# Turning x on VectorE in 32x32 blocks, and centring the weights instead of x

## The chip, the cores and the metric

The kernel runs on one core of a Trainium2 chip. The metric is device microseconds for one execution. TensorE does matmuls and transposes into PSUM, VectorE (DVE) and ScalarE (ACT) move and combine what stands there, GpSimd (POOL) does some elementwise work in SBUF, and SyncE (SP) issues most DMAs, one after the other from one queue.

## What is computed

The reference, cut to what matters here; x is 4 x 1024 x 2048, the context 4 x 64 x 2048, everything float32:

```
h   = layernorm(x)
Q   = h @ Wq.T + bq ;  K = ctx @ Wk.T + bk
att = softmax(Q @ K.T / sqrt(2048)) @ ctx
x1  = x + tanh(g_xattn) * att
h2  = layernorm(x1)
q   = h2 @ fWq.T                               # 64 wide
w   = softmax over the 8 best of 512 slots     # scores of q with aux_keys
aux = (w @ aux_values) @ Wvd.T @ Wvu.T
u   = uncertainty(h2)                          # gelu(h2 @ Wu1.T + bu1) @ Wu2.T, variance, mean log
out = x1 + tanh(g_ffn) * (h2 + gate(u) * aux)
```

## The kernel before

The 4096 tokens are 32 tiles of 128 (8 per batch). Every product in full precision is three matmuls over a high part (rounded to fp32r, made by ScalarE) and a low part (the rest, made by VectorE): `split_product`, lines 46 to 48. The kernel is a row of blocks, each with its own instruction list for every engine; a barrier of the engines stands between blocks.

- `keys_block` (0 to 139.5 us): TensorE turns the context and each of 16 row tiles of Wk (`transpose_group`, line 76: four 128x128 transposes into one PSUM bank), ScalarE and VectorE make high and low parts, 48 matmuls of 256 columns give one tile of the keys' transpose. In the last round the first piece of Wq is converted (lines 222 and 265).
- `score_weights_block` (139.5 to 258.5 us): the score weights are Wq transposed times the keys. For each of 16 column tiles n of Wq, a load brings the 16 pieces of 128 columns of all rows (`load_wq`, two buffers), lines 372 and 402 make the parts, 48 matmuls sum over the rows of Wq into one bank (5.76 us), lines 380 and 409 split the result, and SP stores it. SP alternates loads and stores. Meanwhile POOL subtracts the context's row means (lines 359 and 361), and ScalarE and VectorE split that (390, 417).
- `ffn_block` (258.5 to 304.2 us): 11 jobs turn Wvd, Wvu, the aux values, fWq and the four row tiles of Wu1, and two products are made in between (at jobs 4 and 8). ScalarE takes the jobs' high parts in order (line 596).
- `token_block` (304.2 to about 1021 us): first two context products, then the loop over tiles. x of tile t is loaded (`load_x`), VectorE takes its moments (`bn_stats`, line 1125), ScalarE subtracts the mean (line 958), TensorE turns it in four groups (`turn_x`, line 824), ScalarE and VectorE make the parts xT (lines 963 and 1135). TensorE multiplies xT by the "b" weights (320 columns: 128 of the batch's scores and covariance, 64 of fWq, 128 of Wu1), then by 384 columns of Wu1, then adds the attention's part (lines 911 and 912), which ends a tile.
- `output_block`: loads x again, adds attention and memory parts, and stores. It is bound by its transfers.

The order of the work in the loop is written out by hand, in the function `tile` of each engine; every engine works on the rest of tile t-1 ("late"), on tile t, and on the preparation of tile t+1. On TensorE: b part with the query's transpose of t-1 in its middle, routing scores of t-1, the 384-column part in quarters with the four groups of transposes of x of t+1, the attention's transpose and the slots' transposes between them, slot values, and the attention's part. On VectorE: `late_stats` and `late_scale` (t-1, ends with the hidden layer, line 1185), `late_q_lo`, `late_poly`, scores and softmax of t, `late_slots` (t-1), the low parts of x of t+1 with the moments of t+2 between them, `late_z`. On SP: one load of x per tile, into two buffers; every 8 tiles, after the load of tile 8b+1, it waits for the b part of tile 8b-1 (`S["b_sum"]`), loads the batch's joined b weights (`load_joined_b`, two DMAs of 1 MB into the only buffer), waits for that tile's end and loads the batch's context weights. TensorE waits for the joined weights (`b_in`) at the start of a batch.

```
            with sp.Fori(1, BATCH) as b:
                for k in range(8):
                    sp.wait_ge(S["turned"], G * (8 * b + k - 1))
                    load_x(sp, io, x, x_in, 8 * b + k, k % 2)
                    if k == 1:
                        sp.wait_ge(S["b_sum"], 8 * b)
                        load_joined_b(sp, scr, keep, b)
```

## Time and profile before

| | |
|---|---|
| median of 3 runs | 1194.56 us (1188.38 to 1195.55) |
| profiled execution | 1195.68 us, span 1193.8 us |
| mean granted TensorE clock | 0.971 |
| TensorE matmuls | 1121.9 us busy (94%) |
| VectorE | 749.2 us (63%) |
| ScalarE | 453.6 us (38%) |
| GpSimd | 189.4 us (16%) |
| DMA | 185.28 MB, mean 155 GB/s |

The span runs from the first to the last instruction. Busy time of TensorE counts overlapping matmuls once; its ends are modelled. A wait is put down to the instruction whose semaphore came last. "PEclk" is the share of full clock that was granted.

### The profile page before, as it was taken

To read this page: it belongs to the slowest core of one execution; us is meant where nothing else is said; L and a number is where in the kernel's file an instruction comes from. 1 tells how busy PE (TensorE), PEld (TensorE's weight loads), DVE (VectorE), ACT (ScalarE), POOL (GpSimd) and SP (SyncE) were. 2 spreads that over 40 slices of the span, in tenths; PEclk is the share of its full clock that TensorE was granted. 3 is DMA by queue.
4 is the path that set the end of the run, shared out by engine and by line. 5 is a ranking of instruction groups with operands and counts; after the bars stand their busy time and mean duration, and the time that the engine had idled before them with its cause. 6 is when DMAs were issued, how large, how long until landed. Compare 5 with 4: busy or idle time off the path is not lost. (4 is left out here: it accounts for less than half of the span.)

```text
span 1193.8 us, 21180 instructions
## 1 busy us (share of the span) xinstructions
PE 1121.9 (94%) x7402; PEld 1068.1 (89%) x7402; DVE 749.2 (63%) x1886; ACT 453.6 (38%) x743; POOL 189.4 (16%) x277
## 2 busy tenths in 40 slices
PE   7999889899899999999999999999999994599998
PEld 6999789887899999999999999999999993488886
DVE  6555665446426676767666666667676756777776
ACT  3333314335214343333343343433343423444554
POOL 0000330000001212121212121212222223500000
PEclk9999979899999999999999999999999996799999
DMA  7333449786427711320102320103111117689999
GB/s 282 127 139 138 125 135 303 211 286 268 106 88 195 202 39 67 106 87 35 70 35 70 122 70 35 70 35 121 71 66 40 52 54 167 254 303 390 427 427 390
DMA packets 114647, 185.28 MB, mean 155 GB/s; under 512 B 45876, under 2 KB 95060, under 8 KB 97624
## 3 DMA queue, kind: packets, MB, share of 16 engines
q1 hardware_dynamic: 109432, 147.11, 37.3%
q10 hardware_dynamic: 4608, 33.56, 6.7%
q0 software_dynamic: 576, 4.19, 0.8%
q8 instruction: 19, 0.31, 0.1%
q14 instruction: 12, 0.10, 0.0%
HBM read 140.55 MB, written 54.79 MB: 164 GB/s over the span
## 5 line engine op out<-in xcount | busy, mean ns | idle before, releaser
L46 PE MATMUL tk_hidden_sum<-b_weights,k_turned 128*128 128x384 f32 x512 | 180.0, 352 | 0.0
L48 PE MATMUL tk_hidden_sum<-b_weights,k_turned 128*128 128x384 f32 x512 | 172.4, 337 | 0.0
L47 PE MATMUL tk_hidden_sum<-b_weights,k_turned 128*128 128x384 f32 x512 | 171.5, 335 | 0.0
L46 PE MATMUL tk_b_sum<-b_weights,k_turned 128*128 128x320 f32 (+1 forms) x528 | 166.3, 315 | 0.0
L48 PE MATMUL tk_b_sum<-b_weights,k_turned 128*128 128x320 f32 (+1 forms) x528 | 163.8, 310 | 0.0
L47 PE MATMUL tk_b_sum<-b_weights,k_turned 128*128 128x320 f32 (+1 forms) x528 | 163.4, 309 | 0.0
L963 ACT ACTIVATE k_turned<-tk_bank 128x512 fp32r<-128x512 f32 x128 | 76.5, 598 | 203.0 <-PE tk_bank L76 185.2
L1135 DVE TENSOR_TENSOR k_turned<-tk_bank,k_turned 128x512 fp32r<-128x512 f32 x128 | 88.3, 691 | 66.2 <-ACT k_turned L963 65.8
L46 PEld LDWEIGHTS tk_b_sum<-b_weights,k_turned 128*128 128x128 f32 x528 | 99.2, 188 | 0.3
L47 PEld LDWEIGHTS tk_b_sum<-b_weights,k_turned 128*128 128x128 f32 x528 | 99.3, 188 | 0.0
L48 PEld LDWEIGHTS tk_b_sum<-b_weights,k_turned 128*128 128x128 f32 x528 | 99.1, 188 | 0.0
L47 PEld LDWEIGHTS tk_hidden_sum<-b_weights,k_turned 128*128 128x128 f32 x512 | 96.6, 189 | 1.4
L46 PEld LDWEIGHTS tk_hidden_sum<-b_weights,k_turned 128*128 128x128 f32 x512 | 96.4, 188 | 1.4
L48 PEld LDWEIGHTS tk_hidden_sum<-b_weights,k_turned 128*128 128x128 f32 x512 | 96.1, 188 | 0.0
L46 PE MATMUL sw_mt<-a_KT,a_T 128*128 128x256 f32 x256 | 76.6, 299 | 17.5 <-DVE a_T L402 8.6
L1125 DVE BATCH_NORM_STATS2 tk_stats<-k_rows 128x6 f32<-128x512 f32 x128 | 81.6, 681 | 2.1 <-DMA k_rows<-in_x_dram 2.1
L402 DVE TENSOR_TENSOR a_T<-k_rows,a_T 128x1024 fp32r<-128x1024 f32 x30 | 51.9, 1772 | 48.6 <-ACT a_T L372 48.6
L76 PE MATMUL tk_bank<-k_ident,k_rows 128*128 128x128 f32 x512 | 76.5, 272 | 1.4 <-DVE k_turned L1135 1.4
L46 PE MATMUL ky_keys<-k_turned,a_T 128*128 128x256 f32 x256 | 77.4, 302 | 0.1
L1481 DVE TENSOR_TENSOR k_rows<-k_rows,ob_out 128x512 f32<-128x512 f32 x88 | 59.7, 686 | 27.5 <-PE ob_out L48 23.7
L47 PE MATMUL sw_mt<-a_KT,a_T 128*128 128x256 f32 x256 | 75.8, 296 | 0.0
L48 PE MATMUL sw_mt<-a_KT,a_T 128*128 128x256 f32 x256 | 75.6, 295 | 0.0
(263 smaller groups left out, 2613.2 us busy)
## 6 DMA issues: line engine op xcount, KB each, us to landing
k_rows<-in_x_dram SPq DMA_DIRECT2D x54, 1024.0 KB, 4.9
out_dram<-k_rows ACTq DMA_DIRECT2D x22, 1024.0 KB, 10.6
k_rows<-in_Wk_dram SPq DMA_DIRECT2D x16, 1024.0 KB, 4.8
k_rows<-in_Wq_dram SPq DMA_DIRECT2D x16, 1024.0 KB, 6.5
ob_x<-in_x_dram SPq DMA_DIRECT2D x10, 1024.0 KB, 11.3
out_dram<-ob_x ACTq DMA_DIRECT2D x10, 1024.0 KB, 10.4
b_weights<-scratch_b SPq DMA_DIRECT2D x6, 1024.0 KB, 6.9
scratch_mt<-k_way_out SPq DMA_DIRECT2D x32, 128.0 KB, 2.6
```

The lines of the kernel that those rows point to most:

```text
L46: pe.matmul(out, lh, rh, start=start, stop=False, skip_group_check=skip)
L47: pe.matmul(out, lh, rl, start=False, stop=False, skip_group_check=skip)
L48: return pe.matmul(out, ll, rh, start=False, stop=stop, skip_group_check=skip)
L76: ins = pe.transpose(bank[:, k * rows:(k + 1) * rows], src[0:rows, c * P:(c + 1) * P], ident[0:rows, 0:rows])
L402: dve.tensor_tensor(half(T[u][1], h), half(wq_rows[u], h), f32(half(T[u][0], h)), ALU.subtract).then_inc(lo_done, 1)
L963: act.activation(xT[u][0][:, 4 * g:4 * g + 4, :], bank[g % 2][:].rearrange("p (k n) -> p k n", k=4), ACT.Copy).then_inc(S["x_hi"], 1)
L1125: dve.bn_stats(stats[:, k, :], x[u][:, k * QN:(k + 1) * QN])
L1135: dve.tensor_tensor(xT[u][1][:, 4 * g:4 * g + 4, :], bank[g % 2][:].rearrange("p (k n) -> p k n", k=4), f32(xT[u][0][:, 4 * g:4 * g + 4, : ...
L1481: dve.tensor_tensor(x[s][:, cols], x[s][:, cols], po[n][:], ALU.add).then_inc(S["added"], 1)
```

## The change

- x is no longer centred and no longer turned on TensorE. Every tile is loaded twice: plain (`load_rows`) for the moments, and in blocks (`load_blocks`, four DMAs): partitions 32q to 32q+31 get the columns of quarter q of the rows, four rows of the tile to a partition. VectorE's block transpose then writes four chunks of xT into a PSUM bank, in which row p of chunk c is feature 16p + c. It reads with a step of 16 floats.
- So that this fits, all other operands take the same order of features: the transposes of the context, Wk, fWq and Wu1 on TensorE read every 16th column (`spread=True`).
- To make up for x not being centred, the weights' rows are: for Wq a sum on ScalarE, the negated mean on VectorE, and the mean added in the conversions; for the five jobs of fWq and Wu1 three more ScalarE operations with two drains (`centre`).
- The score weights are made with the loops exchanged: each of 16 row tiles of Wq is loaded whole, with three buffers, and its 48 matmuls add to all 16 results, which stand in the 8 banks of PSUM. All results are split and stored at the end, 4 MB in eight DMAs. `ffn_block` waits for these stores before job 4, since its weights take that memory.
- In the loop, VectorE gets the four block transposes, ScalarE loses the centring, the moments of t+1 instead of t+2 come behind the low parts, and SP waits for the moments of tile t-1 before it loads tile t plainly.

The core of the diff (lines of plumbing, memory and the last tiles left out):

```diff
-def transpose_group(pe, bank, src, g, ident, rows=P):
+def transpose_group(pe, bank, src, g, ident, rows=P, spread=False):
 
     for k in range(4):
         c = 4 * g + k
-        ins = pe.transpose(bank[:, k * rows:(k + 1) * rows], src[0:rows, c * P:(c + 1) * P],
-                           ident[0:rows, 0:rows])
+        part = slice(c, D, KC) if spread else slice(c * P, (c + 1) * P)
+        ins = pe.transpose(bank[:, k * rows:(k + 1) * rows], src[0:rows, part], ident[0:rows, 0:rows])
     return ins
+
+
+def spread(rows):
+
+    return rows.rearrange("p (n c) -> p c n", c=KC)
...
+def wq_slot(n):
+
+    return (2, 0, 1)[n % WQ_RING]
+
+
+def load_wq(sp, io, keep, n):
+
+    sp.dma_start(keep["rows"][wq_slot(n)][:], io["Wq"][n * P:(n + 1) * P, :]).then_inc(keep["wq_in"][n % WQ_RING], 16)
+
+
+def wq_sum(act, keep, n):
+
+    rows = keep["rows"][wq_slot(n)]
+    act.wait_ge(keep["wq_in"][n % WQ_RING], 16 * (n // WQ_RING + 1))
+    return act.activation(rows[:], rows[:], ACT.Copy, accum_out=keep["wq_sum"][:, n:n + 1])
+
+
+def wq_negative_mean(dve, keep, n):
+
+    return dve.tensor_scalar(keep["wq_nmean"][:, n:n + 1], keep["wq_sum"][:, n:n + 1], -1.0 / D, None, ALU.mult)
+
+
+def wq_high(act, keep, n, own):
+
+    return act.activation(keep["T"][n % 2][0][:, own, :], spread(keep["rows"][wq_slot(n)][:])[:, own, :],
+                          ACT.Identity, bias=keep["wq_nmean"][:, n:n + 1])
+
+
+def wq_low(dve, keep, n, own):
+
+    hi, lo = keep["T"][n % 2]
+    return dve.scalar_tensor_tensor(lo[:, own, :], spread(keep["rows"][wq_slot(n)][:])[:, own, :],
+                                    keep["wq_nmean"][:, n:n + 1], f32(hi[:, own, :]), ALU.add, ALU.subtract)
...
+            load_ffn(sp, io, rows, keep["ffn_in"], 0)
+            for n in range(WQ_RING, KC):
+                if n > WQ_RING:
+                    sp.wait_ge(lo_done, 2 * (n - WQ_RING))
+                load_wq(sp, io, keep, n)
+            for n in range(1, FFN_RING):
+                sp.wait_ge(lo_done, 2 * (KC - FFN_RING + n))
+                load_ffn(sp, io, rows, keep["ffn_in"], n)
+            for k in range(KC // 4):
+                sp.wait_ge(out_lo, 2 * k + 2)
                 for part in range(2):
-                    sp.dma_start(scr["mt"][part, :, bass.ds(n, 1), :].rearrange("p o n -> p (o n)"),
-                                 f32(out[u][part])).then_inc(stored[u], 16)
-
-            def body(j, first=False):
-                for u in range(2):
-                    n = 2 * j + u
-                    if not (first and u == 0):
-                        sp.wait_ge(lo_done, 2 * (n - 2))
-                    load_wq(sp, io, rows, rows_in, n, u)
-                    if not (first and u == 0):
-                        store(n - 3, 1 - u)
-
-            body(1, first=True)
-            with sp.Fori(2, KC // 2) as j:
-                body(j)
-
-            for n in range(2):
-                load_ffn(sp, io, rows, keep["ffn_in"], n)
-            store(KC - 3, 1)
-            for u in range(2):
-                sp.wait_ge(lo_done, 2 * (KC - 2 + u))
-                load_ffn(sp, io, rows, keep["ffn_in"], 2 + u)
-                store(KC - 2 + u, u)
+                    sp.dma_start(scr["mt"][part, :, 4 * k:4 * k + 4, :],
+                                 f32(out[part][:, 4 * k:4 * k + 4, :])).then_inc(keep["mt_out"], 16)
...
+            row_sum(1)
+            for n in range(1, KC):
+                if n + 1 < KC:
+                    row_sum(n + 1)
+                weights_hi(n)
...
+            def step(n, u, first=False, last=False):
+                for c in range(KC):
+                    if c % (KC // 2) == 0 and not first:
+                        pe.wait_ge(lo_done, 2 * (n - 1) + c // (KC // 2) + 1)
+                    ins = split_product(pe, bank[c // 2][:, (c % 2) * CR:(c % 2 + 1) * CR],
+                                        (T[u][0][:, c, :], T[u][1][:, c, :]),
+                                        (at(KT[0], n), at(KT[1], n)), first and c % 2 == 0, last, True)
+                    if last and c % 2 == 1:
+                        ins.then_inc(product, 1)
+                if not last:
+                    ins.then_inc(used, 1)
...
+            def centre(n):
+
+                own, r = rows[ffn_buffer(n)], jobs[n][0]
+                act.wait_ge(rows_in[ffn_buffer(n)], 16 * (n // FFN_RING + 1))
+                act.activation(own[0:r, :], own[0:r, :], ACT.Copy, accum_out=row_sum[0:r, :])
+                act.drain()
+                act.activation(row_nmean[0:r, :], row_sum[0:r, :], ACT.Copy, scale=-1.0 / D)
+                act.drain()
+                act.activation(own[0:r, :], own[0:r, :], ACT.Identity,
+                               bias=row_nmean[0:r, 0:1]).then_inc(centred, 1)
+
             for n, (r, dst) in enumerate(jobs):
+                if n + 1 in CENTRED_JOBS:
+                    centre(n + 1)
                 if n == WVU:
                     continue
+                if n == CENTRED_JOBS[0]:
+                    act.wait_ge(keep["mt_out"], MT_STORED)
...
+def load_blocks(sp, io, keep, t):
+
+
+    view = io["x"].rearrange("(t k j) (q f) -> t q j k f", k=P // LANES, j=LANES, q=QUADS)
+    for q in range(QUADS):
+        sp.dma_start(keep["blocks"][q * LANES:(q + 1) * LANES, :].rearrange("j (k f) -> j k f", f=QN),
+                     view[bass.ds(t, 1), q].rearrange("o j k f -> (o j) k f")).then_inc(keep["blocks_in"], 16)
+
+
+def load_rows(sp, io, keep, t):
+
+    sp.dma_start(keep["plain"][:], io["x"].rearrange("(t p) d -> t p d", p=P)[bass.ds(t, 1)]
+                 .rearrange("o p d -> p (o d)")).then_inc(keep["plain_in"], 16)
...
+        def load_tile(sp, t):
+            sp.wait_ge(S["turned"], G * t)
+            load_blocks(sp, io, keep, t)
+            sp.wait_ge(S["mean_var"], t)
+            load_rows(sp, io, keep, t)
...
             with sp.Fori(1, BATCH) as b:
                 for k in range(8):
-                    sp.wait_ge(S["turned"], G * (8 * b + k - 1))
-                    load_x(sp, io, x, x_in, 8 * b + k, k % 2)
+                    load_tile(sp, 8 * b + k)
                     if k == 1:
...
+            def tile(t, u, late=True, late_first=False, last=False):
                 if late:
                     late_square(t - 1)
+                if not last:
+                    x_hi(t + 1, 1 - u, 0)
+                    x_hi(t + 1, 1 - u, 1)
+                if late:
                     late_q_hi(t - 1, late_first)
+                if not last:
+                    x_hi(t + 1, 1 - u, 2)
+                    x_hi(t + 1, 1 - u, 3)
                 soft(t)
                 if late:
                     late_tanh(t - 1)
-                if not last:
-                    x_hi(t + 1, 1 - u, 0)
-                if late:
                     late_exp(t - 1)
-                if not last:
-                    x_hi(t + 1, 1 - u, 1)
                 att_hi(t)
-                if not last:
-                    x_hi(t + 1, 1 - u, 2)
                 if late:
                     late_w_out(t - 1, late_first)
...
+            def turn_x(t, g):
+                dve.transpose(bank[g % 2][:].rearrange("p (c k j) -> p c k j", c=4, j=LANES),
+                              blocks[:].rearrange("p (k i c) -> p c k i", k=P // LANES, c=KC)[:, 4 * g:4 * g + 4]
+                              ).then_inc(S["turned"], 1)
...
+            def tile(t, u, j, late=True, last=False, first=False, second=False):
                 if late:
                     late_stats(t - 1, 1 - u, (j if u else j - 1) // 4, second)
                     late_scale(t - 1, 1 - u)
+                if not last:
+                    turn_ready(t + 1)
+                    turn_x(t + 1, 0)
+                    turn_x(t + 1, 1)
+                if late:
                     late_q_lo(t - 1)
                     late_poly(t - 1)
+                if not last:
+                    x_lo(t + 1, 1 - u, 0)
+                    x_lo(t + 1, 1 - u, 1)
+                    dve.drain()
+                    turn_x(t + 1, 2)
+                    turn_x(t + 1, 3)
                 soft_scores(t, u, j // 4)
                 soft_att(t, u, first or second)
                 if late:
                     late_slots(t - 1)
                 if not last:
-                    x_lo(t + 1, 1 - u, 0)
-                    x_lo(t + 1, 1 - u, 1)
+                    x_lo(t + 1, 1 - u, 2)
+                    x_lo(t + 1, 1 - u, 3)
                 att_lo(t)
                 if late:
                     late_learned(t - 1, 1 - u)
-                if ahead:
-                    moments_of(u, j + 1, (0, 1))
                 if not last:
-                    x_lo(t + 1, 1 - u, 2)
-                if ahead:
-                    moments_of(u, j + 1, (2, 3))
-                    moments(u)
-                if not last:
-                    x_lo(t + 1, 1 - u, 3)
+                    moments(t + 1, 1 - u)
                 if late:
                     late_z(t - 1)
```

## Rows read from the trace of the kernel before

**Rows 1.** Windows: stretch, us, busy of PE, PEld, DVE, ACT, POOL, clock, DMA share, GB/s.

```profile
139.50:258.50 119.00, 100.99 (x768) 99.74 (x768) 62.06 (x49) 38.25 (x48) 21.08 (x6) 0.90 0.71 225
349.00:992.50 643.50, 643.41 (x4254) 633.45 (x4253) 418.44 (x1281) 239.63 (x469) 139.00 (x247) 1.00 0.25 78
1060.00:1193.80 133.80, 128.64 (x590) 105.01 (x588) 100.76 (x239) 63.85 (x52) 0.00 (x0) 1.00 0.99 406
```

**Rows 2.** Timeline of PE, one tile of the loop: start, us, line, operation, count.

```profile
700.55 0.60 PE L76 MATMUL tk_bank<-k_ident,k_rows 128*128 128x128 f32 x4
...
720.62 0.34 PE L48 MATMUL tk_hidden_sum<-b_weights,k_turned 128*128 128x384 f32 x1
720.79 0.60 PE L76 MATMUL tk_bank<-k_ident,k_rows 128*128 128x128 f32 x4
721.14 0.42 PE L46 MATMUL tk_hidden_sum<-b_weights,k_turned 128*128 128x384 f32 x1
721.40 0.34 PE L47 MATMUL tk_hidden_sum<-b_weights,k_turned 128*128 128x384 f32 x1
```

**Rows 3.** Waits of DVE over eight tiles: line, releaser, us, times, longest.

```profile
DVE k_rows L1145 <- PE tk_b_sum L48: 16.5, 8, 2.2
DVE k_turned L1135 <- ACT k_turned L963: 10.8, 16, 1.2
DVE tk_query_stack L1190 <- ACT c_query_ones L980: 8.5, 8, 1.1
DVE k_rows L1180 <- POOL tk_stats L1064: 5.3, 8, 0.7
DVE tk_exp_inv L1152 <- ACT k_rows L968: 4.1, 8, 0.5
```

**Rows 4.** Timeline of DVE in the loop: two moments, one scalar operation.

```profile
706.03 1.28 DVE L1125 BATCH_NORM_STATS2 tk_stats<-k_rows 128x6 f32<-128x512 f32 x2
...
715.62 0.43 DVE L1195 TENSOR_SCALAR k_rows<-k_rows 128x512 f32<-128x512 f32 x1
```

**Rows 5.** Line L1229 (a helper): durations in ns, minimum, median, maximum.

```profile
L1229 DVE TENSOR_TENSOR k_rows<-k_rows x6: 191/192/193, 1008.7 to 1018.9; 128x32 f32<-128x32 f32 x6
...
L1229 DVE TENSOR_TENSOR k_rows<-k_rows,k_stats x2: 214/216/217, 1007.6 to 1020.1; 128x32 f32<-128x32 f32 x2
```

**Rows 6.** Page, groups: line, shapes, count, busy us, mean ns, idle before.

```profile
L963 ACT ACTIVATE k_turned<-tk_bank 128x512 fp32r<-128x512 f32 x128 | 76.5, 598 | 203.0 <-PE tk_bank L76 185.2
```

**Rows 7.** Timeline of SP, issues of the last batch's joined weights.

```profile
819.30 2.06 SPq L673 DMA_DIRECT2D b_weights<-scratch_b  x2
```

**Rows 8.** DMA busy tenths, 40 slices of 0.3 us from 819 us.

```profile
DMA  0000016999999999999999999993111000000000
```

**Rows 9.** Windows of two steps of the score weights, columns as in the first.

```profile
214.80:223.40 8.60, 8.54 (x50) 8.55 (x51) 2.69 (x3) 2.07 (x3) 0.00 (x0) 0.66 0.80 229
223.40:229.10 5.70, 5.70 (x50) 5.70 (x50) 2.70 (x3) 2.27 (x3) 0.00 (x0) 1.00 0.51 158
```

**Rows 10.** Waits of PE, 195 to 262 us.

```profile
PE sw_mt L46 <- DVE k_way_out L409: 8.0, 2, 7.5
```

**Rows 11.** Timeline of ACT, end of the keys stage.

```profile
133.49 1.90 ACT L222 ACTIVATE a_T<-k_rows 128x2048 fp32r<-128x2048 f32 x1
```

**Rows 12.** Timeline of DVE, end of the keys, start of the score weights.

```profile
135.41 2.29 DVE L265 TENSOR_TENSOR a_T<-k_rows,a_T 128x2048 fp32r<-128x2048 f32 x1 [1.36 <-ACT a_T L222]
...
141.27 21.17 DVE L402 TENSOR_TENSOR a_T<-k_rows,a_T 128x1024 fp32r<-128x1024 f32 x4 [1.37 <-ACT a_T L372]
```

**Rows 13.** Timeline of PE: transposes with 64 moving columns.

```profile
270.46 0.64 PE L76 MATMUL fw_bank<-k_ident,k_rows 64*128 64x64 f32 x7
```

**Rows 14.** Groups of ACT in the score-weights stage.

```profile
L372 ACT ACTIVATE a_T<-k_rows 128x1024 fp32r<-128x1024 f32 x30 | 30.1, 1051 | 72.7 <-DMA k_rows<-in_Wq_dram 44.2 <-PE sw_mt L48 26.9 <-PEq L84 1.6
```

**Rows 15.** Timeline of ACT, FFN weights: idle before, releaser.

```profile
280.31 4.46 ACT L596 ACTIVATE b_weights<-fw_bank 128x512 fp32r<-128x512 f32 x8 [7.63 <-PE fw_bank L76]
...
295.03 4.46 ACT L596 ACTIVATE b_weights<-fw_bank 128x512 fp32r<-128x512 f32 x8 [5.43 <-PE fw_av L48]
```

More of the change, by code:

```diff
@@ L374, in step @@
-            def step(n, u, j, first=False, ahead=True):
-                act.wait_ge(product, n + 1)
-                if ahead:
-                    weights_hi(n + 2, u)
-                if not first:
-                    act.wait_ge(stored[u], 32 * j)
-                act.activation(out[u][0], mp[u][:, 0:CR], ACT.Copy).then_inc(out_hi, 1)
-            weights_hi(1, 1)
-            for u in range(2):
-                step(u, u, 0, first=True)
-            for u in range(2):
-                step(2 + u, u, 1)
@@ L387, in _, with row_sum @@
-            act.wait_ge(summed, 1)
-            for u in range(2):
-                step(4 + u, u, 2)
-                act.activation(half(ctxT[0], u), half(cent, u), ACT.Copy).then_inc(cent_hi, 1)
-            with act.Fori(3, KC // 2 - 1) as j:
-                for u in range(2):
-                    step(2 * j + u, u, j)
-            for u in range(2):
-                step(KC - 2 + u, u, KC // 2 - 1, ahead=False)
+            def row_sum(n):
+                wq_sum(act, keep, n).then_inc(row_summed, 1)
@@ new lines, in _ @@
+            for b in range(KC // 2):
+                dve.wait_ge(out_hi, b + 1)
+                dve.tensor_tensor(out[1][:, 2 * b:2 * b + 2, :], bank[b][:].rearrange("p (c n) -> p c n", c=2),
+                                  f32(out[0][:, 2 * b:2 * b + 2, :]), ALU.subtract).then_inc(out_lo, 1)
+        @block.tensor
+        def _(pe):
+            def step(n, u, first=False, last=False):
[9 more added lines that the diff above has]
+                    ins.then_inc(used, 1)
+            step(0, 0, first=True)
+            step(1, 1)
+            with pe.Fori(1, KC // 2 - 1) as j:
@@ L444, in ffn_jobs @@
+            step(KC - 1, 1, last=True)
 def ffn_jobs(io):
@@ L1038, in _ @@
                     tile(2 * j + u, u)
-            tile(TILES - 2, 0, ahead=False)
-            tile(TILES - 1, 1, last=True, ahead=False)
+            tile(TILES - 2, 0)
+            tile(TILES - 1, 1, last=True)
             t = TILES - 1
@@ L1276, in gates @@
                 op(dve.tensor_scalar, keep["f_att"][:], keep["f_x"][:], tgx[:, 0:1], None, ALU.mult)
-            def tile(t, u, j, late=True, last=False, ahead=True, first=False, second=False):
+            def tile(t, u, j, late=True, last=False, first=False, second=False):
                 if late:
@@ L1336, in _ @@
                     tile(2 * j + u, u, j)
-            tile(TILES - 2, 0, PAIRS - 1, ahead=False)
-            tile(TILES - 1, 1, PAIRS - 1, ahead=False, last=True)
+            tile(TILES - 2, 0, PAIRS - 1)
+            tile(TILES - 1, 1, PAIRS - 1, last=True)
             t, u = TILES - 1, 1
@@ L1356, in output_block @@
         RING = OUT_RING
[L1357 removed]
+        x = keep["out_rows"] + [m.sb(f"x{s}", [P, D]) for s in range(FFN_RING, RING)]
         az = [m.sb(f"att_z{u}", [P, 2 * P]) for u in range(2)]
@@ L1529, in gated_cross_attention_and_memory @@
         way_out = m.sb("way_out", [P, 2 * CWN], F32R)
-        keep["mt"] = [[way_out[:, (2 * u + i) * CR:(2 * u + i + 1) * CR] for i in range(2)] for u in range(2)]
+        keep["out_rows"] = keep["rows"][2:] + keep["rows"][:2]
+        keep["blocks"], keep["plain"] = keep["rows"][2:]
         keep["cw_hi"] = [way_out[:, r * CWN:(r + 1) * CWN] for r in range(2)]
```

275 lines of the change are left out of this document (129 added, 146 removed).

## The prediction

> **What bounds the kernel now.** I read the stages first, by windows [rows 1]: TensorE is busy for 643.4 of the 643.5 us of the token loop (349 to 992.5), for 101 of 119 us in the score-weights stage. Then the timeline of TensorE in the loop [rows 2]: the same four transposes stand at 700.55 and at 720.79, so a tile takes 20.24 us, with no gap in it. Then who ends VectorE's idle time over eight such tiles [rows 3]: 16.5 + 10.8 + 8.5 + 5.3 + 4.1 = 45.2 us, 5.65 a tile. So VectorE has 20.23 - 5.65 = 14.58 us of its own per tile (its 0.34 us of issue gaps counted in), and 5.65 us of waits. The loop is TensorE's today; the question is whose it is when work moves from one to the other.
>
> **The loop, TensorE.** Gone are 16 transposes per tile, in 4 groups. A group holds the next matmul back by 0.35 us (720.79 to 721.14), and that one's successor starts 0.26 instead of 0.17 us later, as 720.62 to 720.79 is [rows 2]: 0.44 us a group, 1.78 us a tile, 31 tiles. TensorE alone would need 18.46 us.
>
> **The loop, VectorE.** It gains 4 block transposes of 128x512 and one drain (0.1 us), and loses the negated mean (0.15 us and its gap, 0.23). Own work: 14.58 - 0.23 + 0.1 = 14.45 us. No row shows a block transpose. Lower bound: one 128x512 operation every 0.61 to 0.64 us, as the moments run (two in 1.28 us, [rows 4]); I use 0.61. But each reads x with a step of 16 floats. The nearest rows for a stepped read are two additions over 32 elements, where one input is every fourth float of the statistics: 214 to 217 ns against 191 to 193 ns for the same form with dense inputs [rows 5]. That is 24 ns for 32 elements, 0.75 ns each, 0.39 us for 512: 0.61 + 0.39 = 1.0 us. Upper bound: the dense operation's streaming doubled, 1.15 us. I take 1.0, since a measured row gives it.
>
> By a rule of the Trainium skill (SBUF — State Buffer, "Door 1: The DMA port swizzle") at least two hits on a 16-byte line are needed for full speed, though it also calls a step of four floats free. The rows show a step of four that is not free. Read as half speed, the rule gives 512 more VectorE cycles, 0.53 us by that page's clock for VectorE as an estimate, so 1.14 us per transpose and 17 us more over the loop than my value.
>
> Which waits stay? The order written for VectorE puts transposes 0 and 1 behind the hidden layer's scaling, then waits for ScalarE's rounded query. ScalarE has the square, copy 0, copy 1 and then two small copies: after transpose 1 ends it needs 0.60 (one copy, [rows 6]) and about 0.5, so VectorE waits some 1.15 us, 1.06 today [rows 3]. The waits for the POOL power (5.3/8 = 0.66, call it 0.7) and for the exponential (0.51) stay. The wait for the scores (2.1) and those for ScalarE's copies (1.35) are filled. Period: 14.45 + 0.7 + 1.15 + 0.51 + 4 x 1.0 = **20.8 us**, against 18.46 for TensorE: VectorE becomes the bound, and a tile gets 0.6 us longer, **+19 us** in 31 tiles. With dense price it is 19.25: -31 us; with 1.15 it is 21.4: +36 us. ScalarE also loses its 2 us of centring per tile, which nothing on the path waited for: zero. POOL's first power moves to just behind the moments and takes under 1 us while VectorE finishes the old tile: zero, 0.1 us a tile if that cover is gone. The two loads of x (one in 4 parts, one plain) double about 1 MB a tile; the engines of the DMA are 25% busy in the loop [rows 1]: zero.
>
> **The batch boundaries.** SP is one queue. Before tile 8b it must load the joined weights of batch b, 2 x 1 MB, into the only buffer, after tile 8b-1's own products. Today it issues them as soon as these products end, well before the next tile starts. In the new order the load of tile 8b+1 stands ahead, and its plain half waits for the moments of tile 8b, which are the last but one thing VectorE does in tile 8b-1. So the weights are asked for at about the time TensorE wants them. From the moments M: 0.5 us to wake and issue the plain load; 1 MB of data, 2.7 us at about the 406 GB/s of the last stage [rows 1]; and 9.6 us from the first issue to the last packet of the 2 MB, as in the row at 819.30 and its DMA view [rows 7, 8]. TensorE starts tile 8b at M + 12.8. From there VectorE needs 18.4 us to its next moments (3.8 for the query's transpose, 0.8 to the query's low part, then 13.8 of its listed work and the exponential's wait, without the head of the tile, which it did while TensorE stood). 12.8 + 18.4 - 20.8 = 10.4 us lost. TensorE's clock falls too: after a 7.5 us wait in the score-weights stage it was granted 0.66 over the next 8.6 us, and 50 matmuls took 8.6 instead of 5.7 us [rows 9, 10]: 2.8 us. Together 13.2 us, three times: **+39 us** (low 30 without the clock, high 45 where the loop has its dense price).
>
> **The keys stage.** The order 16p+c wants the whole row, so the first transpose waits for the fourth quarter of the context, and the pipeline behind it starts later: about +2.2 us. At the end the conversion of the first rows of Wq gets a sum ahead of it (2.1 us, as a 1.90 us pass with its readout), a mean (0.15), and stepped reads of 2048 elements on both engines, 1.5 us each at 0.75 ns. ScalarE's pass was 133.49 to 135.39 and VectorE's ended at 137.70, when TensorE had just run out of work [rows 11, 12]: +5.4 us, 2.3 if the step costs nothing. Sum **+7.6** (4.5). TensorE's 288 transposes there take a stepped stationary operand: I price them at nothing, because loads of 128 columns go every 0.07 us ahead of 64-column transposes (7 in 0.64 us, [rows 13]) while the 128-column ones go every 0.11. What it costs otherwise is a rival below.
>
> **The score-weights stage.** The products are as many as before, and the 18.7 us in which POOL shuts VectorE's two-input operation out (141.27, 21.17 us for four, [rows 12]) recur. The 7.5 us wait and its slow clock, 10 us together, came from a queue where loads of 512-byte pieces and stores alternated [rows 9, 10]; with three buffers and whole rows it goes. ScalarE's step becomes 2.1 + 2 x (1.05 + 0.77) = 5.7 us [rows 14], TensorE's is 5.76, so the two copies of the centred context (1.9 each) come out: -10 + 3.8 = **-6 us** (low -10, high +3).
>
> **The second-weights stage** (the block that turns the FFN's weights). 4 MB of score weights, until now stored one piece at a time, leave at the end: at the 406 GB/s of the last stage [rows 1] 10 us, and this stage's small loads and its fifth load stand behind them. ScalarE gets 5 centrings of 2.1 + 1.9 + 0.4 = 4.4 us, 22 us. Its waits for products, 7.6 and 5.4 us [rows 15], cover 13; the rest and 3 us of lateness stay: **+12 us** (low 0, high +28). Ahead of the first tile two groups of transposes go from TensorE: **-1.5 us**.
>
> **Sum.** +7.6 - 6 + 12 - 1.5 + 19 + 39 = +70 us on the profiled execution, 1195.68 us for a span of 1193.8. It lies 1.1 us over the median of 1194.56, so **1265 us**. The output stage is untouched.
>
> **Rivals.** (1) Dense price for the block transposes and copies: +4.5 - 10 + 12 - 1.5 - 31 + 42 = +16, **1211 us**. For it: only two 32-element additions speak of a price. VectorE is still the bound. (2) The step also costs in TensorE's load of the stationary operand: with 0.75 ns for 128 columns, a load every 0.06 to 0.07 becomes one every 0.16 and each transpose 0.05 us longer, 13 us in the 64 groups of the keys; laid on top of the 0.14 us that a load lasts, 32 us. **1290 us.** Nothing in the trace reads by steps there.
> By the Trainium skill (SBUF — State Buffer, same section) such a load would slow too; no run so far shows it.
> (3) Faster: TensorE alone sets the pace. If a block transpose costs under (18.46 - 16.8)/4 = 0.41 us, VectorE's chain fits under TensorE's, everything added on VectorE and ScalarE hides, and the sum is +2.2 - 10 + 0 - 1.5 - 55 + 45 = -19, **1176 us**. The point from which it decides is that 0.41. A dense scalar operation between SBUF tiles does take only 0.43 us for 128x512 [rows 4], so it is not excluded; a write to PSUM and a stepped read speak against it. The removal itself is certain, as no other transposes of x are left.
>
> **Numbers.** Forecast 0.5, rival (1) 0.2, (2) 0.15, (3) 0.1, and 0.05 for sums that land on no change. Within 1% is what a measurement of this kernel cannot tell from no change: 1183 to 1206. Rival (1) reaches into it, so faster 0.10, same 0.10, slower 0.80. The range leaves out rival (3) and the top of (2): 1196 to 1305.
>
> **What would show it.** The block transpose's own duration: near 1.08 us with its latency right, 0.69 rival (1). The period of a tile near 20.8, with TensorE idle behind ScalarE's slot exponential; 19.3 or 18.5 for the others. Three TensorE waits on the joined weights of about 11 us, at tiles 8, 16 and 24, with the clock at its lower level after each. In the keys stage transposes still every 0.11 us. Wrong would be: no wait at the boundaries, or VectorE's chain shorter than its listed parts.

## The result, and the profile after

The changed kernel takes 1275.83 us (median of 4 runs, 1275.3 to 1279.7) against 1194.93 us for the kernel before on the same chip: a ratio of 1.069, 95% interval 1.066 to 1.072. The forecast was 1265 us. Its profiled execution has a span of 1273.5 us, 79.7 more than the 1193.8 of before. The first view to read is the same as in [rows 1], windows by stage, but cut where TensorE starts the first product or transpose of each stage, so that the two kernels can be subtracted row by row. The columns are those of [rows 1]. Before:

```profile
0.00:140.20 140.20, 130.27 (x1063) 127.71 (x1064) 78.30 (x138) 51.53 (x93) 0.84 (x7) 1.00 0.47 165
140.20:260.10 119.90, 101.00 (x769) 99.76 (x769) 61.97 (x48) 38.22 (x48) 21.08 (x6) 0.90 0.71 227
260.10:305.10 45.00, 38.99 (x290) 31.52 (x290) 32.67 (x59) 24.11 (x47) 0.73 (x2) 1.00 0.65 235
305.10:327.50 22.40, 22.40 (x159) 22.36 (x160) 7.02 (x16) 4.02 (x2) 1.60 (x5) 0.92 0.45 105
327.50:980.70 653.20, 651.79 (x4333) 641.89 (x4332) 415.53 (x1266) 239.65 (x466) 138.64 (x245) 1.00 0.25 79
980.70:1024.20 43.50, 18.55 (x93) 15.74 (x91) 27.70 (x78) 13.53 (x23) 12.80 (x9) 0.67 0.55 130
1024.20:1193.80 169.60, 158.89 (x702) 129.14 (x702) 126.00 (x283) 82.57 (x66) 13.73 (x3) 0.96 0.94 382
```

After:

```profile
0.00:147.20 147.20, 130.47 (x1064) 128.95 (x1064) 79.59 (x139) 55.46 (x95) 0.84 (x7) 0.98 0.45 164
147.20:269.20 122.00, 101.14 (x769) 98.95 (x769) 82.95 (x55) 96.80 (x70) 21.72 (x6) 0.92 0.55 205
269.20:329.70 60.50, 45.10 (x290) 39.24 (x290) 34.17 (x61) 43.99 (x67) 0.72 (x2) 0.84 0.59 199
329.70:351.90 22.20, 22.20 (x150) 22.20 (x151) 2.35 (x5) 0.00 (x0) 0.85 (x3) 0.89 0.42 95
351.90:1062.10 710.20, 617.70 (x3829) 593.17 (x3828) 533.55 (x1372) 184.77 (x436) 138.25 (x247) 0.96 0.44 120
1062.10:1104.00 41.90, 17.76 (x94) 15.25 (x92) 27.28 (x79) 13.60 (x23) 12.84 (x9) 0.70 0.57 136
1104.00:1273.50 169.50, 158.96 (x702) 129.19 (x702) 126.31 (x283) 82.44 (x66) 13.71 (x3) 0.96 0.94 381
```

| stage | measured | forecast |
|---|---|---|
| keys | +7.0 | +7.6 |
| score weights | +2.1 | -6 |
| second weights (FFN) | +15.5 | +12 |
| context products | -0.2 | -1.5 |
| tiles | +57.0 | +58 (19 + 39) |
| transition and output | -1.7 | 0 |
| sum | +79.7 | +70 |

TensorE's busy time in the tiles fell from 652 to 618 us, as 504 instructions went (4333 to 3829), and yet the stage grew by 57: TensorE now stands still for 92 us of it. Where it stands shows when the first product of each tile is looked up in the timeline. Before, tiles follow at 20.24 us. After, 27 of the 31 intervals have a mean of 20.52 us (20.4 and 20.7 in turn), together +7.6. The three ahead of tiles 8, 16 and 24 last 32.0 us, together +35.3. The first lasts 53.1 instead of 39.1 us: +14.1, for which the forecast had no term.

**The transpose and the period.** The profile page's group of the block transposes (count, busy us, mean ns of one, idle time before):

```profile
L1170 DVE STREAM_TRANSPOSE tk_bank<-k_rows 128x512 f32<-128x512 f32 x128 | 130.9, 1069 | 14.3 <-DMA k_rows<-in_x_dram 11.1
```

1.07 us in duration, one about every 1.0. VectorE's waits over seven tiles, to be read against [rows 3]: the waits for TensorE's sum and for the copies are gone, the three others are there still, 0.98, 0.74 and 0.51 us a tile.

```profile
DVE tk_query_stack L1234 <- ACT c_query_ones L1025: 6.9, 7, 1.0
DVE k_rows L1224 <- POOL tk_stats L1103: 5.2, 7, 0.8
DVE tk_exp_inv L1196 <- ACT k_rows L1013: 3.6, 7, 0.5
```

**A batch boundary.** First TensorE's timeline about tile 16, and then SP's:

```profile
719.79 0.65 PE L925 MATMUL tk_router<-k_ident,k_rows 128*128 128x128 f32 x4 [1.40 <-ACT k_rows L1033]
...
735.46 0.63 PE L48 MATMUL tk_b_sum<-b_weights,k_turned 128*128 128x320 f32 x1 [11.43 <-DMA b_weights<-scratch_b]
```

```profile
714.14 1.81 SPq L719 DMA_DIRECT2D k_rows<-in_x_dram  x4
723.94 0.35 SPq L725 DMA_DIRECT2D k_rows<-in_x_dram  x1
724.48 4.33 SPq L738 DMA_DIRECT2D b_weights<-scratch_b  x2
```

The first row is the ordinary tile: TensorE idle for 1.4 us behind the slot exponential. The next is the boundary, where TensorE waits 11.4 us for the joined weights. SP shows why: the plain load (L725) waited for the moments and went out at 723.94, and the joined weights (L738) only behind it. TensorE was granted half its clock from 727.1 to 740.8.

**Tile 0.** SP's, VectorE's and TensorE's timelines:

```profile
379.33 0.34 SPq L855 DMA_DIRECT2D scratch_cw<-k_way_out  x1
379.71 0.43 SPq L855 DMA_DIRECT2D scratch_cw<-k_z  x1
380.19 2.01 SPq L719 DMA_DIRECT2D k_rows<-in_x_dram  x4
```

```profile
378.48 0.83 DVE L1368 TENSOR_TENSOR k_z<-k_z,k_way_out 128x640 f32<-128x640 f32 x1 [0.81 <-ACT k_way_out L1066]
390.44 1.97 DVE L1170 STREAM_TRANSPOSE tk_bank<-k_rows 128x512 f32<-128x512 f32 x2 [11.14 <-DMA k_rows<-in_x_dram]
```

```profile
397.80 0.48 PE L953 MATMUL tk_small<-k_ident,k_rows 128*128 128x128 f32 x1 [14.12 <-DVE k_rows L1201]
```

SP stores the second half of the context products, which VectorE finishes at 379.3, and only then asks for tile 1's blocks. VectorE's list has the turning of tile 1 ahead of tile 0's softmax, so it waits 11.1 us for that load, and TensorE waits 14.1 us for tile 0's attention weights.

### The profile page after: what moved, and what is told of

Same layout as the page of the kernel before. It is cut to its first block and busy times, and to the rows that moved or that the text cites. A ratio compares the mean times of both kernels' runs of the same rounds, so it can differ in the third digit from the quotient of the medians.

```text
span 1273.5 us, 20309 instructions
## 1 busy us (share of the span) xinstructions
PE 1093.3 (86%) x6890; PEld 1027.0 (81%) x6890; DVE 886.2 (70%) x1990; ACT 477.1 (37%) x755; POOL 188.9 (15%) x277
## 5 line engine op out<-in xcount | busy, mean ns | idle before, releaser
L48 PE MATMUL tk_b_sum<-b_weights,k_turned 128*128 128x320 f32 (+1 forms) x528 | 169.5, 321 | 35.9 <-DMA b_weights<-scratch_b 34.3
L50 PE MATMUL tk_b_sum<-b_weights,k_turned 128*128 128x320 f32 (+1 forms) x528 | 165.8, 314 | 0.0
L49 PE MATMUL tk_b_sum<-b_weights,k_turned 128*128 128x320 f32 (+1 forms) x528 | 165.8, 314 | 0.0
L1170 DVE STREAM_TRANSPOSE tk_bank<-k_rows 128x512 f32<-128x512 f32 x128 | 130.9, 1069 | 14.3 <-DMA k_rows<-in_x_dram 11.1
L48 PEld LDWEIGHTS tk_b_sum<-b_weights,k_turned 128*128 128x128 f32 x528 | 101.5, 192 | 37.3 <-issue 37.1
L49 PEld LDWEIGHTS tk_b_sum<-b_weights,k_turned 128*128 128x128 f32 x528 | 101.5, 192 | 0.0
L50 PEld LDWEIGHTS tk_b_sum<-b_weights,k_turned 128*128 128x128 f32 x528 | 101.1, 191 | 0.0
L48 PEld LDWEIGHTS tk_hidden_sum<-b_weights,k_turned 128*128 128x128 f32 x512 | 98.7, 193 | 1.5
L49 PEld LDWEIGHTS tk_hidden_sum<-b_weights,k_turned 128*128 128x128 f32 x512 | 97.2, 190 | 1.4
L50 PEld LDWEIGHTS tk_hidden_sum<-b_weights,k_turned 128*128 128x128 f32 x512 | 96.8, 189 | 0.0
L1018 ACT ACTIVATE k_rows<-k_rows 128x512 f32<-128x512 f32 x32 | 20.2, 632 | 201.7 <-DVE k_rows L1229 201.7
L1179 DVE TENSOR_TENSOR k_turned<-tk_bank,k_turned 128x512 fp32r<-128x512 f32 x128 | 82.6, 686 | 16.6 <-ACT k_turned L1008 15.5
L344 DVE SCALAR_TENSOR_TENSOR a_T<-k_rows,a_wq_nmean,a_T 128x1024 fp32r<-128x1024 f32 (+1 forms) x31 | 75.2, 2444 | 26.3 <-ACT a_T L337 26.3
L48 PE MATMUL sw_mt<-a_KT,a_T 128*128 (+1 forms) x256 | 76.8, 300 | 16.4 <-DVE a_T L344 15.7
L1165 DVE BATCH_NORM_STATS2 tk_stats<-k_rows 128x6 f32<-128x512 f32 x128 | 79.0, 680 | 0.0
L256 DVE TENSOR_TENSOR a_T<-ky_bank,a_T 128x512 fp32r<-128x512 f32 x64 | 43.7, 690 | 46.2 <-ACT a_T L219 45.6
## 6 DMA issues: line engine op xcount, KB each, us to landing
out_dram<-ob_x ACTq DMA_DIRECT2D x10, 1024.0 KB, 10.2
```

Of the source, the lines that this page charges most:

```text
L48: pe.matmul(out, lh, rh, start=start, stop=False, skip_group_check=skip)
L49: pe.matmul(out, lh, rl, start=False, stop=False, skip_group_check=skip)
L50: return pe.matmul(out, ll, rh, start=False, stop=stop, skip_group_check=skip)
L256: dve.tensor_tensor(T[u][1][:, 4 * g:4 * g + 4, :], bank[g][:].rearrange("p (k n) -> p k n", k=4), f32(T[u][0][:, 4 * g:4 * g + 4, :]), AL ...
L344: return dve.scalar_tensor_tensor(lo[:, own, :], spread(keep["rows"][wq_slot(n)][:])[:, own, :], keep["wq_nmean"][:, n:n + 1], f32(hi[:, o ...
L1165: dve.bn_stats(stats[:, k, :], plain[:, k * QN:(k + 1) * QN])
```

## The experiments

Theory: VectorE's chain sets the period, the order on SP's queue makes the stall at a boundary, and the stepped reads are what the block transposes cost over a dense pass. The rivals are in each expectation. The edits are shown shortened. Differences in us are against the 1275.83 of the kernel after; each ratio is against runs of the kernel before that were made beside that run (medians 1195.2 to 1196.5 us).

**e1.** At k == 1 of each batch:

```
-  load_tile(sp, 8 * b + 1)      # blocks, wait mean_var, rows
-  sp.wait_ge(S["b_sum"], 8 * b); load_joined_b(sp, scr, keep, b)
+  sp.wait_ge(S["turned"], G * (8 * b + 1)); load_blocks(sp, io, keep, 8 * b + 1)
+  sp.wait_ge(S["b_sum"], 8 * b); load_joined_b(sp, scr, keep, b)
+  sp.wait_ge(S["mean_var"], 8 * b + 1); load_rows(sp, io, keep, 8 * b + 1)
```

> The kernel after, but before tiles 8, 16 and 24 the joined weights are requested ahead of the plain half of the next load of x, so they no longer stand behind the wait for the moments. Theory (SP's order): TensorE's three waits for the joined weights (34.3 us in all, longest 11.5) go, and the three tiles that last 32 us shrink to about 20.6: 3 x 11.4 = 34 us, 1242 us. Rival (the transfer): 2 MB and the plain megabyte have to come in the same stretch whatever the order; then the moments of the next tile come late instead, VectorE waits for its plain half, and 0 to 15 us are gained: 1261 to 1276 us.

Measured: 1252.38 us, ratio to before 1.046 (1.044 to 1.049), 23 us less than after. TensorE's and SP's timelines at tile 8:

```profile
556.64 0.41 PE L48 MATMUL tk_b_sum<-b_weights,k_turned 128*128 128x320 f32 x1 [3.30 <-DMA b_weights<-scratch_b]
```

```profile
543.46 1.81 SPq L719 DMA_DIRECT2D k_rows<-in_x_dram  x4
545.45 4.99 SPq L738 DMA_DIRECT2D b_weights<-scratch_b  x2
```

The wait is 3.3 instead of 11.5 us, since the request still stood behind the wait of the blocks. Boundary tiles last 23.9 us. The result lies between the theory and the rival, and e10 separates them. The clock also fell for less time: half of it was granted for 3.4 us at each boundary, against 10.2 to 13.7 us in the kernel after.

**e10.** The joined load ahead of the blocks as well:

```
+  sp.wait_ge(S["b_sum"], 8 * b); load_joined_b(sp, scr, keep, b)
   sp.wait_ge(S["turned"], G * (8 * b + 1)); load_blocks(sp, io, keep, 8 * b + 1)
-  sp.wait_ge(S["b_sum"], 8 * b); load_joined_b(sp, scr, keep, b)
```

> The kernel after, with the joined weights requested as soon as the products that use the old ones are done, ahead of both the blocks and the plain rows of tile 8b+1. With the blocks still ahead (run e1) TensorE waited 3.3 us at each boundary. Theory (only the time of the request counts): the request comes 3 to 4 us sooner, the wait is gone, the boundary tiles last about 21 instead of 32 us: -33 us, 1243 us. Rival (the 2 MB then delay the blocks of tile 8b+1, for which VectorE waits in order): the gain stays at e1's 24 us, 1252 us.

Measured: 1241.79 us, ratio 1.037 (1.033 to 1.042), 34 us less than after. SP's timeline before tile 8:

```profile
534.42 2.65 SPq L738 DMA_DIRECT2D b_weights<-scratch_b  x2
537.66 3.90 SPq L719 DMA_DIRECT2D k_rows<-in_x_dram  x4
```

Requested at 534.4 and landed at 543.4, the weights are there 4 us before tile 8 starts; the intervals at the boundaries are 20.4 and 20.5 us, and the clock is whole from 401 to 1043 us. From the first request to the last landing the blocks took 10.2 us there (7.4 in the next tile), and no interval grew. So the 35 us of the boundaries, the lower clock in them included, come from the order on SP's queue.

**e3.** ScalarE's order alone:

```
   x_hi(t + 1, 1 - u, 0)
-  x_hi(t + 1, 1 - u, 1)
   late_q_hi(t - 1, late_first)
+  x_hi(t + 1, 1 - u, 1)
```

> The kernel after, with ScalarE's order alone changed: the rounded query is made before the copy of block transpose 1, not behind it. No work is added or removed. Theory (VectorE's chain sets the period): its wait for the query, 0.98 us a tile, falls to about 0.2, the period from 20.55 to about 19.8, 28 tiles of it: -21 us, 1255 us, and TensorE's idle time of 1.4 us ahead of the slot weights' transposes falls by the same. Rival (TensorE or the chain through ScalarE's exponential sets the period, VectorE's wait is slack): the wait reappears behind it, 1276 us.

Measured: 1251.03 us, ratio 1.044 (1.041 to 1.048), 25 us less. The mean period is 19.6 us; VectorE's wait for the query no longer appears among its waits, and TensorE's for the exponential fell from 1.4 to 0.9 us a tile (six tiles):

```profile
PE tk_router L925 <- ACT k_rows L1033: 5.4, 6, 1.1
```

Taking 0.98 us of wait from VectorE took 0.9 from the period: VectorE is the bound.

**e5.** Dense reads in `turn_x` (this kernel leaves out the right order of the features):

```
-  blocks[:].rearrange("p (k i c) -> p c k i", k=P // LANES, c=KC)[:, 4 * g:4 * g + 4]
+  blocks[:].rearrange("p (c k i) -> p c k i", k=P // LANES, c=KC)[:, 4 * g:4 * g + 4]
```

> The kernel after, with one part of the computation changed: each block transpose of x in the loop reads 512 neighbouring floats of a row instead of every 16th pair of blocks, so the features come in the wrong order and the output is not the reference's. Shape, type and count of the operations are the same. Theory (the stepped read is what costs): 1.07 us falls to about 0.69, four a tile are 1.5 us, the period would be 19.0 and is held up at 19.1 to 19.2 by TensorE, whose tile is 20.55 - 1.4 us: 28 x 1.4 = 39 us less, 1237 us. Rival (the block transpose or its write to PSUM costs it): 1.07 us stay, 1276 us.

Measured: 1234.52 us, ratio 1.033 (1.030 to 1.037), 41 us less; the period is 19.1 us. The profile page's group:

```profile
L1170 DVE STREAM_TRANSPOSE tk_bank<-k_rows 128x512 f32<-128x512 f32 x128 | 84.3, 704 | 12.9 <-DMA k_rows<-in_x_dram 9.8
```

The step costs 0.365 us of 1.069 for 512 floats, 0.71 ns each. The price of 0.75 ns that two operations of 32 elements with a step of four floats showed [rows 5] held, nearly, for a step of 16 floats in an operation sixteen times as long. With dense reads the changed kernel would still be slower than before.

**e6.** Order alone, so that all three of VectorE's waits are filled:

```
 VectorE:  late_stats, turn_x(0), late_scale, turn_x(1), late_q_lo, late_poly,
           x_lo(0), x_lo(1), turn_x(2), turn_x(3), soft_scores, x_lo(2), soft_att, ...
 ScalarE:  x_hi(0), late_square, late_q_hi, x_hi(1), x_hi(2), x_hi(3), soft, ...
```

> The kernel after, with the order alone changed so that all three waits of VectorE's are filled: block transpose 0 goes between the statistics and the scaling (over POOL's power), the rounded query comes ahead of copy 1 on ScalarE, low part 2 goes between the scores' minimum and the exponential's sum. Theory (VectorE's chain sets the period): its waits of 2.2 us a tile (0.98, 0.73, 0.50) go, its own work is 20.55 - 2.2 = 18.35, and TensorE, which keeps a gap of 0.54 in 19.1 with the dense read, holds the period at about 18.6: 28 x 1.95 = -55 us, 1221 us. Rival (the filled waits open others, as the query's path through TensorE and ScalarE is now longer): 19.4 us, -32 us, 1244 us.

Measured: 1226.11 us, ratio 1.026 (1.024 to 1.027), 50 us less. The period is 18.6 us. VectorE's longest regular wait over seven tiles, and TensorE's window:

```profile
DVE tk_att_stack L1206 <- ACT tk_att_stack L1029: 2.8, 7, 0.4
```

```profile
580.00:700.00 120.00, 119.68 (x760) 117.01 (x758) 108.00 (x282) 37.08 (x88) 27.77 (x52) 1.00 0.42 113
```

TensorE is busy for 119.7 of 120 us, so its own work bounds the tile again, at 18.6 us; the forecast put that at 18.46.

**e2.** The order of tile 0 alone:

```
   SP, r == 1:
+  load_tile(sp, 1)
   sp.wait_ge(S["cw_low"], 2)
   VectorE, tile 0:
-  turn_ready(1), turn_x and x_lo of tile 1, soft_scores, soft_att, x_lo, att_lo, moments
+  soft_scores, soft_att, att_lo, turn_ready(1), turn_x and x_lo of tile 1, moments
   ScalarE, tile 0:
-  x_hi(1, 1, 0 to 3), soft(0), att_hi(0)
+  soft(0), att_hi(0), x_hi(1, 1, 0 to 3)
```

> The kernel after, with two changes of order for tile 0 alone: SP requests the loads for tile 1 before it waits for the second context store, and VectorE and ScalarE do tile 0's scores and attention weights before they turn tile 1. Theory (a load at the end of SP's queue with VectorE waiting for it in order): the 14.1 us for which TensorE stands at 397.8, behind attention weights that VectorE reaches only after tile 1's blocks have landed, go but for some 2 us that turning tile 1 still needs: -12 us, 1264 us. Rival (tile 1's blocks are simply late, one buffer for them): TensorE waits as long for tile 1 instead, -2 to -5 us, 1271 to 1274 us.

Measured: 1273.17 us, ratio 1.065 (1.062 to 1.067); its interval overlaps that of after. Tile 0 is down from 53.1 to 38.0 us, but tile 1 is up from 19.8 to 26.2:

```profile
400.87 0.47 PE L912 MATMUL tk_small<-k_ident,k_rows 128*128 128x128 f32 x1 [4.55 <-DVE k_rows L1234]
```

The result is nearer to the rival. Tile 1's blocks cannot be requested before tile 0's are turned (377.8 here), because there is one buffer, and what was a wait for a load becomes VectorE's own backlog. 8.8 us of 14.1 came back over both tiles; in the profiled execution 2.8 us of that went in the stages ahead and 1.7 about the boundaries, which the edit does not touch.

**e4.** Four buffers instead of three for the rows of Wq:

```
-WQ_RING = 3
+WQ_RING = 4
-    return (2, 0, 1)[n % WQ_RING]
+    return (3, 0, 1, 2)[n % WQ_RING]
-            load_ffn(sp, io, rows, keep["ffn_in"], 0)
-            for n in range(1, FFN_RING):
+            for n in range(FFN_RING):
```

> The kernel after, with four buffers instead of three for the rows of Wq in the score-weights stage; the first load of the next stage waits in return. Theory (the ring is the bound): a row's buffer is asked for again when its low part is done, and from there load 5.3, sum 1.9, two halves of the row before 4.1, sum of the next 1.9, own halves 4.1, last low half 2.05 make 19.35 us for three steps, 6.45 each, as measured (6.44). With four the bound is ScalarE's own 1.9 + 0.1 + 4.1 = 6.0 us: 0.4 us in some 12 steps, and the wait of 12.2 us for row 4 behind VectorE's slow first rows shrinks: -5 to -9 us, 1267 to 1271 us. Rival (ScalarE is the bound already, its waits are slack): 1276 us.

Measured: 1272.04 us, ratio 1.065 (1.062 to 1.068): not separable from after in the total. The stage itself is 115.9 instead of 122.0 us. ScalarE's timeline, after and then e4:

```profile
220.50 1.92 ACT L327 ACTIVATE k_rows<-k_rows 128x2048 f32<-128x2048 f32 x1 [1.55 <-DMA k_rows<-in_Wq_dram]
...
222.41 4.00 ACT L337 ACTIVATE a_T<-k_rows,a_wq_nmean 128x1024 fp32r<-128x1024 f32 x2
...
233.37 1.92 ACT L327 ACTIVATE k_rows<-k_rows 128x2048 f32<-128x2048 f32 x1 [1.09 <-DMA k_rows<-in_Wq_dram]
```

```profile
216.02 1.90 ACT L327 ACTIVATE k_rows<-k_rows 128x2048 f32<-128x2048 f32 x1
...
217.92 4.07 ACT L337 ACTIVATE a_T<-k_rows,a_wq_nmean 128x1024 fp32r<-128x1024 f32 x2
221.90 1.90 ACT L327 ACTIVATE k_rows<-k_rows 128x2048 f32<-128x2048 f32 x1
```

With three buffers every second sum waits for its load in this stretch and two steps take 12.9 us (220.50 to 233.37); with four a step is 5.88 us (216.02 to 221.90), ScalarE's own work. So in this steady part of the stage the ring of three was the bound.

**e8.** In `centre` of the FFN block:

```
-  act.activation(own, own, ACT.Copy, accum_out=row_sum); drain
-  act.activation(row_nmean, row_sum, ACT.Copy, scale=-1.0 / D); drain
-  act.activation(own, own, ACT.Identity, bias=row_nmean).then_inc(centred, 1)
+  act.activation(row_nmean, own[:, 0:1], ACT.Copy, scale=-1.0 / D).then_inc(centred, 1); drain
```

> The kernel after without the centring of the five blocks of FFN weights: ScalarE's pass for the row sum and its pass that subtracts the mean are left out, so the output is not the reference's. Theory (ScalarE's 22 us of centring, 13 of them hidden): the stage, 60.5 us against 45.0 before, gets 9 to 13 us shorter, 1263 to 1267 us. Rival (the 4 MB of score weights stored at the end and the loads queued behind them set the stage): at most 5 us, 1271 us or more.

Measured: 1267.28 us, ratio 1.060 (1.058 to 1.062). The stage's window:

```profile
269.70:317.80 48.10, 42.59 (x290) 36.98 (x290) 33.76 (x61) 25.08 (x52) 0.73 (x2) 0.92 0.74 251
```

12.4 of the 15.5 us that the stage gained are the centring, 3.1 are not. The whole run gained less, 8.6 us (9.8 in the profiled executions), as the other stages came out 2.6 us longer. TensorE's clock has a part in both numbers: its 290 instructions were busy for 39.0 us at a granted 1.00 before, 45.1 at 0.84 after and 42.6 at 0.92 here. So up to 3.6 us of what is left here, and up to 6.1 of the 15.5, can be slower products; how much of that bound the stage was not tested.

**e7.** The edits of e6, e2, e4 and e10 together, and

```
-  wq_high(act, keep, 0, slice(0, KC)).then_inc(next_hi, 1)
+  for h in range(2):
+      wq_high(act, keep, 0, slice(h * KC // 2, (h + 1) * KC // 2)).then_inc(next_hi, 1)
```

with VectorE's `wq_low` in the same halves.

> All together: the order of e6, tile 0 as in e2, a ring of four rows of Wq, the joined weights requested right behind the products that use the old ones, ahead of both loads of tile 8b+1, and the conversion of the first rows of Wq in two halves, so that VectorE's half overlaps ScalarE's. Theory (the terms are independent): 1276 - 55 (order) - 34 (boundaries) - 12 (tile 0) - 4 (ring, measured) - 2 (halves) = 1169 us, 0.98 of the kernel before. Rival (TensorE is now the bound, so what was hidden in VectorE's slack at the boundaries and at the clock comes out): 1190 to 1200 us, no gain over the kernel before.

Measured: 1178.68 us, ratio to before 0.985 (0.983 to 0.986). Its window from the first product of tile 0 to the last of tile 31:

```profile
346.80:965.20 618.40, 605.03 (x3829) 592.48 (x3828) 529.05 (x1372) 185.37 (x436) 138.41 (x247) 0.99 0.51 138
```

618 us against 653 before and 710 after. That is nearer to the theory of independent terms than to the rival. The terms add up all but 10 us: tile 1 lasts 28.3 us, boundary intervals 20.2 to 21.0 instead of 18.6.

**e9.** e7, with tile 1's order of VectorE and ScalarE as it was in after, and on VectorE, for four of the five centred blocks (n + 2):

```
+  dve.tensor_reduce(row_sum[:, k:k + 1], rows[ffn_buffer(n + 2)][:], AX.X, ALU.add); drain
+  dve.tensor_scalar(row_nmean[:, k:k + 1], row_sum[:, k:k + 1], -1.0 / D, None, ALU.mult)
   ScalarE, centre(n):
-  sum, drain, scale, drain
+  act.wait_ge(mean_up, k)
```

> The kernel e7 with two more changes of order: VectorE sums the rows of four of the five centred blocks of FFN weights, two blocks ahead, so that ScalarE is left with one pass for each; and in tile 1 VectorE scales tile 0 before it turns tile 2, as in the kernel after. Theory (ScalarE's chain sets the second-weights stage): four sums of 2.4 us leave it, 5 to 8 us come out of the 61.8 us of the stage, and tile 1, 28.3 us long, gives back about 2: 1169 to 1172 us against 1178.7. Rival (the sums now hold up VectorE's low parts, which TensorE's next transposes wait for): no gain in the stage, 1177 us.

Measured: 1175.30 us, ratio 0.983 (0.980 to 0.986), which overlaps e7's. Tile 1 gave back 2.8 us, the stage 1.6 (61.8 to 60.2): freeing ScalarE of four sums hardly shortens it, against the 5 to 8 us of the theory. What bounds it then was not tried.

## Why the prediction was right, and where it was not

**The bound of the loop: right.** VectorE's chain took over from TensorE, by e3 and e6. The block transposes cost nearly what the 32-element rows said, by e5. (Those two operations are multiplications, not additions as the prediction calls them: the arithmetic is in `gates`.) The period came out 0.3 us shorter than 20.8: waits of 2.2 instead of 2.36 us, own work of 18.3 instead of 18.45. The forecast's own 20.81 less 20.24, 31 times, is 18 us and not 19. TensorE alone needs 18.6, by e6.

**The boundaries: right in mechanism and place, a little large in size.** The forecast had TensorE start at M + 12.8. The plain load, which goes out as the moments end, went at 723.94 and TensorE started at 735.46, 11.5 us on. From TensorE's start to the next moments VectorE took 20.3, 21.1 and 20.1 us; forecast were 18.4 and 2.8 for the clock. 35.3 us were measured against the old period of 20.24, which is 34.4 against the new one, as the forecast counts; 39 were forecast, and e10 took 34.8 out of the three intervals.

**Tile 0: missed, 14.1 us.** The prediction walked through SP's queue at batch boundaries but not at the start, where tile 1's load stands behind the context stores. It is made up by the two terms above, 19 us of which only 7.6 (27 tiles) came and 39 of which 35.3 came. So it was luck that the +58 for the tiles met the measured +57.0. The same holds for the total: terms that came out larger than forecast add up to 27 us (tile 0, both weight stages and the context products), those that came out smaller to 17, and the 10 us between +70 and +79.7 are what is left.

**The score-weights stage: the term that was mis-sized, by 8 us.** The forecast was -6, measured +2.1. The step that failed is that ScalarE's step of 5.7 us stays under TensorE's 5.76 "with three buffers". Two things stood in its place. ScalarE's stepped halves take 2.0 us, not 1.82, so its step is 5.88; and the time from the end of a row's low part, through its buffer's next load, to the low part of the row three on is longer than three steps. The ring of four gives back 6.1. Another 3 us are where the stages were cut: the stores of the score weights hold the next stage's start, TensorE waits 5.2 instead of 2.2 us there, and the forecast had booked that in the next stage. SP issued the last of these stores from 267.5 to 268.8 us, and TensorE's next transposes began at 269.2.

**The second-weights stage: right in kind, small.** Centring costs 12.4 us, forecast 9 (22 less 13 hidden). For the late stores 3 us were forecast. Those 3 at the stage's head are theirs; the other 3.1 are not shown to be, as the lower clock (e8) can account for them. The forecast had no term for the clock in this stage.

**The context products: -0.2 against -1.5.** Nine instructions went (159 to 150), but the granted clock was 0.89 instead of 0.92, so TensorE was busy for 22.2 us against 22.4.

**The keys stage: +7.0 against +7.6, by other parts than forecast.** ScalarE's and VectorE's timelines at its end, to be read against [rows 11, 12]:

```profile
134.47 1.90 ACT L327 ACTIVATE k_rows<-k_rows 128x2048 f32<-128x2048 f32 x1
...
136.69 3.77 ACT L337 ACTIVATE a_T<-k_rows,a_wq_nmean 128x2048 fp32r<-128x2048 f32 x1 [0.22 <-DVE a_wq_nmean L332]
```

```profile
140.48 3.68 DVE L344 SCALAR_TENSOR_TENSOR a_T<-k_rows,a_wq_nmean,a_T 128x2048 fp32r<-128x2048 f32 x1 [3.83 <-ACT a_T L337]
```

VectorE is done at 144.2 instead of 137.7, 6.5 us later (5.4 forecast, beside 2.2 for the later start). The start is 4.3 us later (8.3 against 4.0), but the first products of the keys begin at 17.1 against 17.2 before: that delay was hidden.

**Rival (2), the stepped stationary operand: its price is 5 ns, not 50.** Weight loads of the keys' transposes in the kernel before, then after (ns, minimum, median, maximum):

```profile
L76 PEld LDWEIGHTS ky_bank<-k_ident,k_rows x236: 139/140/142, 21.2 to 131.0; 128*128 128x128 f32 x118
```

```profile
L79 PEld LDWEIGHTS ky_bank<-k_ident,k_rows x236: 192/196/203, 20.4 to 132.0; 128*128 128x128 f32 x118
```

The load does last 56 ns longer, yet transposes follow at 114 instead of 109 ns, since a load lies beside the transpose before it. So the load does slow with a step, as the prediction's last sentence on this rival expects, but little of it shows. The last key product ends 1.0 us later. Rival (1) is out by e5's comparison, rival (3) because a transpose takes 1.07 us and not 0.41. Once the waits are filled, as in e6 and e7, TensorE does set the pace, as rival (3) had it, at 18.6 us a tile, but by taking out waits and not by a cheaper transpose.

**The step's price.** The transposes lose 0.365 us to a step of 16 floats. The Trainium skill (SBUF — State Buffer, "Door 1: The DMA port swizzle"), read as half speed, gave 0.53 us as an estimate. The direction agrees, and the measured price is lower.

## What to carry to other kernels

In this kernel, work moved from a full engine to a half-idle one paid only once the order was right too. Filling the waits in the new bound's chain was worth 50 us and SP's queue 34, and e7, which has both, is 1.5% faster than the kernel before. What left TensorE shortens its own tile by 1.6 us (20.24 to 18.6). When a load is split or moved on a queue, walk the queue once for the steady state, once for each boundary and once for the first pass: a load behind a wait for another engine can be late by that wait. Price a ring of buffers as a loop (load, every operation until release) divided by its depth, not by the slowest engine alone.

## What was not expected of the hardware

- A stepped read costs about the same per element on VectorE in three kinds of operation. With a step of 16 floats it is 0.71 ns in the block transpose (1.069 against 0.704 us for 512) and 0.68 in a subtraction of 2048 (3.68 against 2.29 us; the stepped one also adds the mean). With a step of 4 floats it is 0.75 in the two small operations of [rows 5]. On ScalarE a step of 16 costs 0.86 ns: 3.77 us for 2048, against 2.00 for the dense operation of the same form in `centre`.
- A weight load for a transpose lasts 196 instead of 140 ns with such a step, and 51 of these 56 ns are hidden.
- One 128x512 block transpose of fp32 into PSUM takes 0.70 us with dense reads, about as long as the moments of 512 floats (0.68).
- TensorE was granted half its clock for 10.2 to 13.7 us at each boundary where it had waited 11.4 us, and for 17.1 us about the 14.1 us wait of the first tile; after the 3.3 us of e1's tile 8 its products ran at their usual 0.31 us for 1.4 us and then at half the clock for 3.4 (558.1 to 561.5, 0.47 us each). After the waits of 1.4 us in ordinary tiles the clock stayed whole.
